# Node sums from exact halves: one-hot stationary, messages moving, sums copied and turned; second load of x moved

## The reference

```
xn  = layernorm(x)
e   = edge_attr_128 @ W_edge + b_edge          # 50000 x 256
msg = relu(xn[src] + e)
agg = segment_sum(msg, dst)                    # 3125 x 256
h   = (1 + eps) * xn + agg
h   = relu(h @ W1 + b1) @ W2 + b2              # then batch norm, relu, added to x
```

## Time and profile before

| | us |
|---|---|
| median of 3 runs | 1014.28 (1013.24 to 1014.35) |
| the profiled execution's own time | 1009.37 |
| its span, first to last instruction | 1007.6 |
| start to the first gather, 0 to 43 | 43.0 |
| first gather to the end of the edge stage | 43.0 to 560 |
| behind the edge stage | 447.6 |

### The profile page before, as it was taken

How to read it: one execution, slowest core, us unless ns; L and a number is a source line. 1 busy time by engine, 2 the same in 40 slices (tenths; PEclk the granted TensorE clock), 3 DMA queues, 4 the chain that set the end, 5 groups by cost and what they waited for, 6 DMA issues and landing times.

```text
span 1007.6 us, 17432 instructions
## 1 busy us (share of the span) xinstructions
PE 926.4 (92%) x6055; PEld 824.6 (82%) x6055; DVE 601.8 (60%) x1098; ACT 538.3 (53%) x1064; POOL 544.6 (54%) x527
## 2 busy tenths in 40 slices
PE   5899999999999999999999975379999999999995
PEld 4677889889888888897888765368999999999994
DVE  5555665565665565568989778835554454555442
ACT  2744545445545455445545564836555666555552
POOL 3277777777777777777774004023444444444433
PEclk8899999999999999999999998589999999999998
DMA  9667888877878878799775105459799789888722
GB/s 247 198 165 231 264 259 266 254 253 251 277 243 260 274 252 262 249 304 324 248 241 184 43 1 182 168 201 384 236 312 308 239 289 301 279 253 301 244 42 28
DMA packets 93173, 234.59 MB, mean 233 GB/s; under 512 B 20425, under 2 KB 37843, under 8 KB 84122
## 3 DMA queue, kind: packets, MB, share of 16 engines
q1 hardware_dynamic: 56694, 116.95, 33.9%
q0 software_dynamic: 29136, 64.72, 26.5%
q10 hardware_dynamic: 7252, 51.75, 12.8%
HBM read 183.81 MB, written 50.23 MB: 232 GB/s over the span
## 4 chain that ended last, share of the span: by engine, by line
PE 59%; POOL 13%; DMA 10%; DVE 8%; issue 7%; ACT 2%; DVEq 0%; POOLq 0%; SPq 0%; ACTq 0%
PE banks L1154 15%; POOL work L775 13%; PE banks L1174 10%; DMA work<-node_table,srcT 8%; PE banks L476 7%; PE banks L450 7%; PE banks L1176 5%; PE banks L924 3%; PE banks L983 2%; PE banks L439 2%; PE banks L1063 2%; PE banks L1051 1%; DVE work L526 1%; PE banks L1138 1%; DMA wts<-in_src 1%
## 5 line engine op out<-in xcount | busy, mean ns | idle before, releaser
L775 POOL DMA_INDIRECT work<-node_table,srcT x391 | 382.9, 979 | 151.6 <-issue 109.8
L498 ACT ACTIVATE work<-work 128x512 f32<-128x512 f32 x195 | 120.9, 630 | 127.0 <-DVE work L526 126.3
L476 PEld LDWEIGHTS banks<-work 128*128 128x128 f32 x1560 | 184.2, 192 | 4.5 <-DVE hT L544 1.1
L476 PE MATMUL banks<-work 128*128 128x128 f32 x1560 | 184.8, 275 | 0.7 <-DVE hT L544 0.7
L450 PE MATMUL banks<-w_edge,eaT 128*128 128x256 f32 x780 | 179.1, 379 | 0.0
L526 DVE TENSOR_TENSOR work<-banks,work 128x512 f32<-128x512 f32 x195 | 128.0, 682 | 69.5 <-DMA work<-node_table,srcT 55.1
L824 POOL DMA_INDIRECT out<-work,row_i x54 | 86.5, 1601 | 141.5 <-ACT work L1444 118.9
L1154 PE MATMUL banks<-xe_hi,wup 128*128 128x256 f32 x864 | 158.8, 285 | 3.8 <-DVE xe_lo L1901 3.8
L450 PEld LDWEIGHTS banks<-w_edge,eaT 128*128 128x128 f32 x780 | 143.1, 190 | 17.0 <-issue 0.2
L1174 PE MATMUL banks<-wdown,hid_hi 128*128 x432 | 155.9, 403 | 0.0
L1909 DVE TENSOR_TENSOR hid_lo<-wts,hid_hi 128x512 fp32r<-128x512 f32 x108 | 72.4, 691 | 134.7 <-ACT hid_hi L1421 134.7
(11 more groups left out here) (258 smaller groups left out, 1199.1 us busy)
## 6 DMA issues: line engine op xcount, KB each, us to landing
wup<-split_table ACTq DMA_DIRECT2D x24, 2048.0 KB, 9.7
work<-in_edge_attr SPq DMA_DIRECT2D x65, 384.0 KB, 5.1
wts<-in_L_ffn_W SPq DMA_DIRECT2D x64, 256.0 KB, 4.6
split_table<-raw_hi SPq DMA_DIRECT2D x64, 256.0 KB, 2.6
split_table<-raw_lo SPq DMA_DIRECT2D x64, 256.0 KB, 4.2
wdown<-split_table SPq DMA_DIRECT2D x8, 2048.0 KB, 9.7
work<-node_table,srcT POOLq DMA_INDIRECT x391, 4.5
wup<-split_table SPq DMA_DIRECT2D x3, 2048.0 KB, 8.2
```

The costliest lines, as they stand in the source:

```text
L476: last = nc.tensor.matmul(bank[5][:, h * P:(h + 1) * P], msg[:, u, j, h * P:(h + 1) * P], onehot[:, u, j], start=(j == 0), stop=(j == GT - 1))
L498: nc.scalar.activation(msg[:, u, 2 * q:2 * q + 2], msg[:, u, 2 * q:2 * q + 2], ACT.Relu).then_inc(msg_ready, 1)
L775: pool.indirect_dma_start(out=xg[i % RING][0:rows, j % 2], out_offset=None, in_=node_table, in_offset=bass.IndirectOffsetOnAxis(ap=srcT[0: ...
```

## The change

The messages are split into two float32r parts whose sum is the message: ACT's relu now writes the high part (msg_hi, placed where x stood), and a new DVE instruction for each group, low_messages, writes the low one (max(msg, 0) - msg_hi). Both operands of it and its result are in SBUF, 128 x 1536. PE now holds the one-hot stationary and streams 256 columns of a part, 12 products a group in float32r. The sums come out with nodes on partitions, so ACT copies them to SBUF (copy_sums), PE turns them (turn_sums, two 128 x 128 transposes), and DVE adds the turned sums; all of that two groups later. In PE's loop aggregate moves from ahead of the attention's products to behind them. In DVE's loop add_window moves from the group's start to between its second and third add. The second load of x moves behind the edge stage, since x's place is in use until then.

```diff
-        onehot = view(work, 7680, 2, GT, P)
+        msg_lo = nc.alloc_sbuf_tensor_at("msg_lo", [P, 2, GT, DIM], F32R, offset=work_offset + 4 * 4608)
+        msg_hi = nc.alloc_sbuf_tensor_at("msg_hi", [P, 2, GT, DIM], F32R, offset=xs_offset)
+        sums = xs[:, 12]
+        onehot = nc.alloc_sbuf_tensor_at("onehot", [P, 2, GT, P], F32R, offset=work_offset + 4 * 7680)
...
-        def aggregate(pe, n, u, fresh=False):
+        def aggregate(pe, n, u, fresh=False, tiles=GT):
             if not fresh:
                 pe.wait_ge(agg_read, n)
             pe.wait_ge(onehot_ready, n + 1)
+            pe.wait_ge(msg_low, n + 1)
+            for j in range(tiles):
+                for m in (msg_hi, msg_lo):
+                    last = nc.tensor.matmul(bank[5][:, 0:DIM], onehot[:, u, j], m[:, u, j],
+                                            start=(j == 0 and m is msg_hi), stop=(j == tiles - 1 and m is msg_lo))
+            last.then_inc(agg_ready, 1)
+
+        def turn_sums(pe, n):
+            pe.wait_ge(sums_copied, n + 1)
             for h in range(HALVES):
-                for j in range(GT):
-                    if h == 0 and j % 2 == 0:
-                        pe.wait_ge(msg_ready, PAIRS * n + j // 2 + 1)
-                    last = nc.tensor.matmul(bank[5][:, h * P:(h + 1) * P], msg[:, u, j, h * P:(h + 1) * P], onehot[:, u, j],
-                                            start=(j == 0), stop=(j == GT - 1))
-            last.then_inc(agg_ready, 1)
+                last = nc.tensor.transpose(bank[5][:, DIM + h * P:DIM + (h + 1) * P], sums[:, h * P:(h + 1) * P], ident[:])
+            last.then_inc(turned, 1)
...
+        def copy_sums(act, n):
+            act.wait_ge(agg_ready, n + 1)
+            nc.scalar.copy(sums, bank[5][:, 0:DIM]).then_inc(sums_copied, 1)
...
+        def high_messages(act, n, u):
             for q in range(PAIRS):
                 act.wait_ge(sums_done, PAIRS * n + q + 1)
-                nc.scalar.activation(msg[:, u, 2 * q:2 * q + 2], msg[:, u, 2 * q:2 * q + 2], ACT.Relu
-                                     ).then_inc(msg_ready, 1)
+                nc.scalar.activation(msg_hi[:, u, 2 * q:2 * q + 2], msg[:, u, 2 * q:2 * q + 2], ACT.Relu
+                                     ).then_inc(msg_high, 1)
+
+        def low_messages(dve, n, u, tiles=GT):
+            dve.wait_ge(msg_high, PAIRS * (n + 1))
+            nc.vector.scalar_tensor_tensor(out=msg_lo[:, u, 0:tiles], in0=msg[:, u, 0:tiles], scalar=0.0,
+                                           in1=msg_hi[:, u, 0:tiles].bitcast(F32), op0=ALU.max, op1=ALU.subtract
+                                           ).then_inc(msg_low, 1)
...
-                c = n - 2 * TILES - 1
-                if 0 <= c < CHUNKS:
-                    for d, s in node_rows(a["x"], xs[:, c * CHUNK_TILES:(c + 1) * CHUNK_TILES], c):
-                        sp.dma_start(s, d).then_inc(x_again, 16)
...
             sp.wait_ge(edges_done, 1)
+            for c in range(CHUNKS):
+                for d, s in node_rows(a["x"], xs[:, c * CHUNK_TILES:(c + 1) * CHUNK_TILES], c):
+                    sp.dma_start(s, d).then_inc(x_again, 16)
...
+                if n >= 2:
+                    turn_sums(pe, n - 2)
                 if n == DEN0:
                     attn_weights()
-                if n >= 1:
-                    aggregate(pe, n - 1, (n - 1) % 2, n == 1)
...
+                if n >= 1:
+                    aggregate(pe, n - 1, (n - 1) % 2, n == 1)
...
+            act.wait_ge(rows_ready, CHUNKS)
             for n in range(GROUPS):
+                if n >= 2:
+                    copy_sums(act, n - 2)
                 if n + 1 < GROUPS:
                     copy_group(n + 1)
...
                 if n >= 2:
-                    add_window(dve, n - 2, starts[(n - 2) % GT], mixed_by(n + 1), n == 2)
+                    dve.wait_ge(agg_ready, n - 1)
...
+                if not last:
+                    add_nodes(dve, n, n % 2, range(PAIRS - 1))
+                if n >= 2:
+                    add_window(dve, n - 2, starts[(n - 2) % GT], mixed_by(n + 1), n == 2)
...
+                    add_nodes(dve, n, n % 2, (PAIRS - 1,))
...
                 if n >= 3:
                     round_low(dve, n - 3)
+                low_messages(dve, n, n % 2, 1 if last else GT)
```

More of the change, by code:

```diff
@@ L117, in build @@
         qT = sb("qT", [P, HALVES, NODES_PAD])
+        xs_offset = next_offset()
         xs = sb("xs", [P, TILES, DIM])
@@ L307, in build @@
         sums_done = sem("sums_done")
-        msg_ready = sem("msg_ready")
+        msg_high = sem("msg_high")
+        msg_low = sem("msg_low")
+        sums_copied = sem("sums_copied")
+        turned = sem("turned")
         onehot_ready = sem("onehot_ready")
@@ L489, in copy_tail, with high_tail @@
             nc.scalar.copy(eaT[:, u, 0], eaT_out[:, 0, 0:P]).then_inc(eaT_ready, 1)
[L491 removed]
+        def copy_sums(act, n):
+            act.wait_ge(agg_ready, n + 1)
+            nc.scalar.copy(sums, bank[5][:, 0:DIM]).then_inc(sums_copied, 1)
+        def high_tail(act, n, u):
             act.wait_ge(sums_done, PAIRS * (n + 1))
[L493 to L495 removed]
+            nc.scalar.activation(msg_hi[:, u, 0], msg[:, u, 0], ACT.Relu).then_inc(msg_high, PAIRS)
+        def high_messages(act, n, u):
             for q in range(PAIRS):
                 act.wait_ge(sums_done, PAIRS * n + q + 1)
[L498 to L499 removed]
+                nc.scalar.activation(msg_hi[:, u, 2 * q:2 * q + 2], msg[:, u, 2 * q:2 * q + 2], ACT.Relu
[5 more added lines that the diff above has]
+                                           ).then_inc(msg_low, 1)
         def mark_window(dve, g, u):
@@ L519, in add_tail, with add_nodes @@
             nc.vector.tensor_tensor(msg[:, u, 0], bank[2][:, 0:DIM], xg[i % RING][:, 0], ALU.add).then_inc(sums_done, PAIRS)
-        def add_nodes(dve, n, u):
-            for q in range(PAIRS):
+        def add_nodes(dve, n, u, pairs=range(PAIRS)):
+            for q in pairs:
                 i = PAIRS * n + q
@@ L538, in add_window @@
         def add_window(dve, n, start, mixed, fresh=False):
-            dve.wait_ge(agg_ready, n + 1)
+            dve.wait_ge(turned, n + 1)
             if not fresh:
@@ L543, in add_window @@
             w = hT[:, :, bass.ds(start, WINDOW)]
-            nc.vector.tensor_tensor(w, bank[5][:, 0:DIM].rearrange("p (h c) -> p h c", h=HALVES),
+            nc.vector.tensor_tensor(w, bank[5][:, DIM:2 * DIM].rearrange("p (h c) -> p h c", h=HALVES),
                                     w, ALU.add).then_inc(agg_read, 1)
@@ L1014, in _ @@
                     attn_den((n - DEN0) // 2)
+                if n >= 1:
+                    aggregate(pe, n - 1, (n - 1) % 2, n == 1)
                 if n >= DEN0 + 3 and (n - DEN0 - 3) % 2 == 0:
                     attn_out((n - DEN0 - 3) // 2)
-            aggregate_tail(pe, GROUPS - 1, (GROUPS - 1) % 2)
+            turn_sums(pe, GROUPS - 2)
+            aggregate(pe, GROUPS - 1, (GROUPS - 1) % 2, tiles=1)
+            turn_sums(pe, GROUPS - 1)
             again = pe.value_load(miss_i[0:1, 0:1], min_val=0, max_val=1)
@@ L1030, in _ @@
                         aggregate(pe, n, 0)
+                        turn_sums(pe, n)
             with pe.Else():
@@ L1306, in _ @@
                 if n < GROUPS - 1:
-                    relu_messages(act, n, n % 2)
+                    high_messages(act, n, n % 2)
                 else:
-                    relu_tail(act, n, n % 2)
+                    high_tail(act, n, n % 2)
                 if n == 2 * TILES:
@@ L1321, in _ @@
                     nc.scalar.copy(w2_hi[:], w2[:]).then_inc(w12_high, 1)
+            for n in range(GROUPS - 2, GROUPS):
+                copy_sums(act, n)
             again = act.value_load(miss_i[0:1, 0:1], min_val=0, max_val=1)
@@ L1327, in _ @@
                         copy_edges(act, n, 0, False, 1)
-                        relu_messages(act, n, 0)
+                        high_messages(act, n, 0)
+                        copy_sums(act, n)
             with act.Else():
@@ L1644, in _ @@
                 else:
-                    add_nodes(dve, n, n % 2)
+                    add_nodes(dve, n, n % 2, (PAIRS - 1,))
                 if n % 2 == 0 and 2 <= n <= 2 * TILES:
@@ L1689, in _ @@
                         add_nodes_again(dve, n)
+                        low_messages(dve, n, 0)
                         add_window(dve, n, w * WINDOW, TILES)
```

1 line of the change is left out of this document (removed).

## The result

The changed kernel takes **1088.92 us** (median of 4 runs, 1087.89 to 1095.96) against 1014.25 before: 1.0752 times as long, 95% interval 1.0723 to 1.0781. Slower was forecast, 1067 in a range of 1038 to 1100. The profiled execution took 1088.0 us with a span of 1086.3, 78.7 more than before.

A forecast was written before the change was run, and what follows sets the result against it. The prediction took POOL's unbroken string of gathers as the bound, PE nearly level. 42 (held gathers) + 13 (DVE in groups 52 to 64) - 2 (load of x) = +53 us gave 1067, range 1052 to 1092, widened to 1038 to 1100.

The forecast's parts named there:

- POOL is the bound, PE's gain is worth nothing: Edge stage to group 51: POOL issues gathers without pause, so PE's gain of about 0.85 us a group doesn't show.
- The hold: 0.81 us a group, +42: Groups up to 448 us: low_messages holds one POOL gather a group until it ends, 0.81 us on average, +42 us.
- The sentence that it isn't quite random: Gathers meet low_messages at phases shaped by L587 right ahead, so the hold was taken as 0.81 us, not 0.97.
- No hold (rival): Gathers are not held by DVE; POOL keeps its pace and only DVE's 13 us remain: 1025 us, chance 0.12.
- DVE's own time, 13 us behind group 51: Groups 52 to 64: with low_messages DVE takes 8.9 us a group against 7.88, +13 us.
- DVE becomes the bound there: Groups 52 to 64: DVE at 8.9 us a group sets the pace, POOL with 7.5 + 0.9 stays below.
- from group 52 on DVE without idle: Sign that the forecast is right: DVE never idles in groups 52 to 64.
- The moved order "costs nothing": Aggregate behind the attention's products: the chain of 14.8 us a pair stays below POOL's 17, so no cost.
- The remark that a lowered clock would make the sum too small: Edge stage: if new idle times of 1 to 2 us lowered PE's clock, PE could bind again; no size given.
- The order on PE (rival, 0.08): The pair's chain over PE, ACT and DVE is really 18 us or more and binds: 1100 to 1110, chance 0.08.
- The load of x, -2: Second load of x out of the loop spares group 51's last add part of its gather wait: -2 us.
- The end of the stage, 0: After group 64's last add: low_messages, shorter sum, copy and turn twice, within 2 us of before, taken as 0.

The follow-up runs named there:

- b_low: The kernel before plus only the new DVE instruction, its result unread, and the second load of x behind the edge stage: 1063.85 us, 1.0504.
- a_best: The changed kernel with window, turn and aggregate early, and low_messages as three 128x512 instructions in a row: 1028.87 us, 1.0142.
- a_early: The changed kernel with DVE's window at the group's start, turn ahead of the next edges, aggregate ahead of the products: 1065.28 us, 1.0505.
- a_busy: The changed kernel with products that nobody reads filling PE's idle places: 1081.41 us, 1.0667.
- a_thirds: The changed kernel with low_messages as three 128x512 instructions, the first ahead of the window: 1076.24 us, 1.0624.
- b_xmove: The kernel before with only the second load of x moved behind the edge stage: 1010.96 us, 0.9986.
- a_psum: The changed kernel with low_messages' second input from PSUM in groups 3 to 49, so node sums differ: 1124.63 us, 1.1108; group 51 38.9 us earlier.

## Why the prediction was right, and where it was not

- **POOL is the bound, PE's gain is worth nothing.** Right: aggregate got shorter, PE's busy time up to group 51 fell, and no time came of it in any run.
- **The hold: 0.81 us a group, +42.** Right in mechanism and size: 0.82 in the trace, 38.9 us taken back by moving one input to PSUM. The sentence that it isn't quite random was needed too; 0.97 would have given 50. How the moments fall differs from order to order: in groups 0 to 51 the holds add up to 44.9 us in the changed kernel and 38.1 in b_low.
- **No hold (rival).** False: the wait is where the second input lies in SBUF, for a 1.76 us instruction as for those of 0.68.
- **DVE's own time, 13 us behind group 51.** Right where DVE is what binds: 13.5 in b_low, 13.2 in a_best. In the changed kernel DVE was busy only 113 of 135 us there: the step "DVE becomes the bound there" failed, and with it the sign "from group 52 on DVE without idle".
- **The moved order "costs nothing".** This step failed. Its chain was worked out for the even groups of the first 52 and stopped there. It left out that aggregate waits for agg_read, the window of the group before, and that this window now stands behind two adds: window, aggregate, the attention's output, the next edges, embed and two adds form a loop behind group 51. PE stands up to 6.3 us in it, its clock falls, and the loop gets longer. It costs 19 us (135.1 against 115.8 in a_early). The wait starts it, since both the wait and the lowered clock are gone with the early order; how much of the 19 us the clock makes stays open, and by the rows under a_busy it can be most of them. The remark that a lowered clock would make the sum too small named this, with no price.
- **The range held by luck in part.** 1088.9 lies inside 1052 to 1092 although 22 us of it are not in the sum: the room was meant for the size of the hold and of DVE's own time, which needed hardly any of it, and the order used it.
- **The order on PE (rival, 0.08)** had 18 us a pair up to group 51 as its point. It did not bind there, but a_thirds, with 0.68 us more ahead of the window, shows how near it was. The forecast was too sure of its 2 us to spare.
- **The load of x, -2.** The reason is false: the late landing stays without it. The size can't be told: b_xmove's interval is -3.2 to +0.5 us.
- **The end of the stage, 0.** 3.6 us, of which 1.9 come back with the early order (11.3 in a_early). The other 1.7 are not the second copy and turn, for b_low, which has neither, takes 11.3 too: they come with low_messages. The 1.5 us behind the stage were not looked into.

## What to carry to other kernels

An engine whose issuing is not counted as busy can be the bound: look at the string of its instructions and ask what in a new instruction elsewhere touches it, above all one longer than the string's spacing, which catches one every time. Here splitting it into three took back 40 of 75 us with more work in all. When an instruction that frees a buffer is moved behind other work, follow the semaphore it raises to everyone who waits, in each phase of the loop and not only in the longest one.

## What the runs showed of the hardware

A gather issued by POOL is held by a DVE instruction with two inputs in SBUF, to 0.82 us behind its end, and not at all by one of the same length with one input in PSUM (a_psum). The Trainium skill states in "SBUF — State Buffer", section "Who interferes with whom", that a VectorE instruction with two SBUF inputs contends with a GpSimd instruction that reads SBUF, and the trace agrees. It infers there that tensor_tensor spares descriptor generation; for these indirect gathers, which take their indices from SBUF, the trace shows otherwise (1.45 us beside a tensor_tensor). New to me was how much waits of 3.6 us on PE cost beyond themselves: L936 took 3.78 instead of 1.88 us, and aggregate with the attention's output 7.12 instead of 4.52.
